# Layer 1 of a two-layer graph network: the fp16 halves of the attention probabilities formed per head from the exponentials, without a normalised fp32 copy

## The reference, cut to what matters

```python
def _L1_gnn_ref(x, adjacency_mask, Wq, Wk, Wv, Wo, bo):     # HEADS = 4, DIM_HEAD = 64
    q, k, v = split_heads(x @ Wq), split_heads(x @ Wk), split_heads(x @ Wv)
    sim = einsum('bhid,bhjd->bhij', q, k) * scale
    sim = where(adjacency_mask[:, None], sim, neg)
    attn = softmax(sim, axis=-1)
    out = einsum('bhij,bhjd->bhid', attn, v) ...
    return out @ Wo + bo
# x: (128 graphs, 128 nodes, 512).  Layer 0 (another attention, 8 heads) comes first:
x = x + _L0_gnn_ref(relu(layernorm(x)), adj, ...)
x = x + _L1_gnn_ref(relu(layernorm(x)), adj, ...)
```

## Time and profile before

| | |
|---|---|
| time, median of 3 runs | 2702.32 us (2700.8 to 2704.07) |
| the profiled execution | 2702.11 us, its span 2700.3 us |
| layer 1 in the trace | from about 1811 us to the end |
| busy over the span | PE 2599.2 us (96%), DVE 1982.8 (73%), ACT 1751.2 (65%), POOL 1403.3 (52%) |
| mean granted TensorE clock | 0.982 |

### The profile page before, as it was taken

One profiled execution on the slowest core, in us unless ns is written; L12 is line 12 of the kernel. 1 busy time (PEld: TensorE's weight loads), 2 busy tenths in 40 slices (PEclk: granted clock), 3 DMA queues, 4 the chain that ended last, 5 costly groups with the idle time before them and its releaser, 6 DMA issues. The chain is left out here.

```text
span 2700.3 us, 62494 instructions
## 1 busy us (share of the span) xinstructions
PE 2599.2 (96%) x20882; PEld 1398.8 (52%) x20886; DVE 1982.8 (73%) x6359; ACT 1751.2 (65%) x5020; POOL 1403.3 (52%) x2798
## 2 busy tenths in 40 slices
PE   7999999999999999999999999947999999999998
PEld 3455555555555555555555555533555555555554
DVE  5477777777777877777777778655777777777765
ACT  3566666666666666666666666645777777777774
POOL 4254555455545555555555455514655656555552
PEclk9999999999999999999999999968999999999998
DMA  4367666766766676667666766675777877777773
GB/s 139 66 142 150 134 135 142 147 131 135 150 146 136 131 150 147 129 138 154 139 132 140 155 128 131 120 174 113 159 165 160 171 163 165 167 159 170 155 149 91
DMA packets 944336, 385.33 MB, mean 143 GB/s; under 512 B 857488, under 2 KB 859024, under 8 KB 944016
## 3 DMA queue, kind: packets, MB, share of 16 engines
q1 hardware_dynamic: 944016, 381.34, 66.7%
HBM read 112.76 MB, written 67.11 MB: 67 GB/s over the span
## 5 line engine op out<-in xcount | busy, mean ns | idle before, releaser
L535 ACT ACTIVATE probs<-probs,negmax 128x128 f32<-128x128 f32 x1024 | 398.2, 390 | 468.4 <-DVE negmax L121 468.4
L446 POOL TENSOR_TENSOR o_sb<-o_sb,xres 128x512 f32<-128x512 f32 x128 | 162.7, 1271 | 503.5 <-DVE o_sb L694 498.3
L163 PE MATMUL ps_pj<-wm_hi,hT 128*128 128x512 f16 x1024 | 326.6, 381 | 14.2 <-DVE m_sb L637 7.3
L163 PE MATMUL ps_pj<-wv_hi,hT 128*128 128x512 f16 x1024 | 326.4, 380 | 0.0
L163 PE MATMUL ps_pj<-hT,wk_hi 128*128 128x512 f16 x1024 | 305.8, 380 | 0.0
L163 PE MATMUL ps_pj<-hT,wq_hi 128*128 128x512 f16 x1024 | 304.5, 379 | 0.0
L1231 ACT ACTIVATE l_probs<-l_probs,l_negmax 128x128 f32<-128x128 f32 x512 | 199.1, 390 | 153.8 <-DVE l_negmax L121 153.8
L1167 POOL TENSOR_TENSOR l_h<-l_h 128x512 f16<-128x512 f32 x124 | 143.6, 1158 | 271.7 <-ACT l_h L1210 190.8
L121 DVE CUSTOM_DVE_ANT_0 probs<-ps_sc,mask 128x128 f32<-128x128 f32 x1024 | 235.5, 284 | 52.2 <-PE ps_sc L900 52.2
L676 DVE SCALAR_TENSOR_TENSOR c<-cprobs,c 128x512 f16<-128x512 f32 x256 | 183.0, 715 | 81.2 <-ACT c L542 81.1
L542 ACT ACTIVATE c<-cprobs 128x512 f16<-128x512 f32 x256 | 160.3, 626 | 122.0 <-DVE cprobs L670 118.3
(11 more groups left out here) (197 smaller groups left out, 6665.8 us busy)
## 6 DMA issues: line engine op xcount, KB each, us to landing
xg<-in_x SPq DMA_DIRECT2D x128, 256.0 KB, 3.3
xres<-in_x SPq DMA_DIRECT2D x128, 256.0 KB, 3.0
x_scratch<-o_sb SPq DMA_DIRECT2D x128, 256.0 KB, 2.4
out<-l_o_sb SPq DMA_DIRECT2D x128, 256.0 KB, 3.3
room<-x_scratch SPq DMA_DIRECT2D x124, 256.0 KB, 3.1
cpT<-c SPq DMA_TRANSPOSE x256, 3.2
hT<-h SPq DMA_TRANSPOSE x128, 3.3
mask_u<-in_adj SPq DMA_DIRECT2D x32, 64.0 KB, 2.4
```

The costliest lines, as they stand in the source:

```text
L163: last = pe.matmul(out, a(kt), b(kt), start=(n == 0), stop=(n == 3 * kts - 1))
L446: nc.gpsimd.tensor_tensor(o_sb[:, j % 2], o_sb[:, j % 2], xres[:, j % 2], ALU.add).then_inc(res_done, 1)
L535: last = nc.scalar.activation(probs[:, i], probs[:, i], ACT.Exp, bias=negmax[:, u % 2, i:i + 1], scale=-1.0, accum_out=zsum[:, u % 4, hh:h ...
```

## The change

The multiplication by the reciprocal moves out of `normalise` into the two steps that write fp16. `normalise` becomes `reciprocals`: one small operation scales the four row sums by 2^-14, a second takes the reciprocal, with a semaphore wait between them. `p_high` becomes four instructions, one per head, that read `probs` with the head's reciprocal as a per-partition scale. `p_low` becomes four instructions of the same kind. The tile `nprobs` and its semaphore `np_done` go; `probs` and `rec` get two buffers, and `row_max(n)` now waits for `p_low(n-2)`.

```diff
-        rec = sb("rec", [P, HB])
-        probs = sb("probs", [P, HB, P])
-        nprobs = sb("nprobs", [P, HB, P])
+        rec = sb("rec", [P, 2, HB])
+        probs = sb("probs", [P, 2, HB, P])
...
             def exps(n):
                 act.wait_ge(negmax_done, count(n + 1))
-                act.wait_ge(np_done, count(n))
                 for hh in range(HB):
-                    last = nc.scalar.activation(probs[:, hh], probs[:, hh], ACT.Exp, bias=negmax[:, n % 2, hh:hh + 1], scale=-1.0,
+                    last = nc.scalar.activation(probs[:, n % 2, hh], probs[:, n % 2, hh], ACT.Exp, bias=negmax[:, n % 2, hh:hh + 1], scale=-1.0,
                                                 accum_out=zsum[:, n % 2, hh:hh + 1])
                 last.then_inc(exp_done, 1)
 
             def p_high(n):
-                act.wait_ge(np_done, count(n + 1))
+                act.wait_ge(rec_done, count(2 * n + 2))
                 act.wait_ge(pT_loaded[n % 2], 16 * (n // 2))
-                nc.scalar.activation(p16[:, n % 2, 0], nprobs[:], ACT.Copy, scale=F16_SCALE).then_inc(phi_done, 1)
+                for hh in range(HB):
+                    last = nc.scalar.activation(p16[:, n % 2, 0, hh], probs[:, n % 2, hh], ACT.Copy, scale=rec[:, n % 2, hh:hh + 1])
+                last.then_inc(phi_done, 1)
...
             def row_max(n):
                 if n % QUAD == 0:
                     dve.wait_ge(mask_ready, count(n // QUAD + 1))
-                dve.wait_ge(np_done, count(n))
-                mask_scores(nc, dve, s_ready, count(n + 1), probs, ps_s, mask[:, n // QUAD % 2, n % QUAD],
+                dve.wait_ge(plo_done, count(n - 1))
+                mask_scores(nc, dve, s_ready, count(n + 1), probs[:, n % 2], ps_s, mask[:, n // QUAD % 2, n % QUAD],
                             negmax[:, n % 2]).then_inc(negmax_done, 1)
 
-            def normalise(n):
+            def reciprocals(n):
                 dve.wait_ge(exp_done, count(n + 1))
-                nc.vector.reciprocal(rec[:], zsum[:, n % 2]).then_inc(rec_done, 1)
-                dve.wait_ge(rec_done, count(n + 1))
-                nc.vector.tensor_tensor(nprobs[:], probs[:], rec[:].unsqueeze(2).to_broadcast([P, HB, P]),
-                                        ALU.mult).then_inc(np_done, 1)
+                nc.vector.tensor_scalar(rec[:, n % 2], zsum[:, n % 2], 1.0 / F16_SCALE, None, ALU.mult).then_inc(rec_done, 1)
+                dve.wait_ge(rec_done, count(2 * n + 1))
+                nc.vector.reciprocal(rec[:, n % 2], rec[:, n % 2]).then_inc(rec_done, 1)
 
             def p_low(n):
                 dve.wait_ge(phi_done, count(n + 1))
-                nc.vector.scalar_tensor_tensor(p16[:, n % 2, 1], nprobs[:], F16_SCALE, p16[:, n % 2, 0], ALU.mult,
-                                               ALU.subtract).then_inc(plo_done, 1)
+                for hh in range(HB):
+                    last = nc.vector.scalar_tensor_tensor(p16[:, n % 2, 1, hh], probs[:, n % 2, hh], rec[:, n % 2, hh:hh + 1],
+                                                          p16[:, n % 2, 0, hh], ALU.mult, ALU.subtract)
+                last.then_inc(plo_done, 1)
```

More of the change, by code:

```diff
@@ L1075, in layer1 @@
             sem(n) for n in ("relu_done", "hhi_done", "q_done", "k_done", "vhi_done", "exp_done", "phi_done", "ahi_done")]
-        hlo_done, vlo_done, negmax_done, rec_done, np_done, plo_done, alo_done, out_done = dve_sems = [
-            sem(n) for n in ("hlo_done", "vlo_done", "negmax_done", "rec_done", "np_done", "plo_done", "alo_done", "out_done")]
+        hlo_done, vlo_done, negmax_done, rec_done, plo_done, alo_done, out_done = dve_sems = [
+            sem(n) for n in ("hlo_done", "vlo_done", "negmax_done", "rec_done", "plo_done", "alo_done", "out_done")]
         mask_ready, res_ready = pool_sems = [sem("mask_ready"), sem("res_ready")]
@@ L1356, in _ @@
             row_max(0)
-            normalise(0)
+            reciprocals(0)
             p_low(0)
@@ L1368, in _ @@
                 if n + 1 < B:
-                    normalise(n + 1)
+                    reciprocals(n + 1)
                 if n + QUAD < B:
```

## The result

| | before | after |
|---|---|---|
| time, median of 5 runs | 2701.71 us (2698.89 to 2704.07) | 2713.73 us (2710.13 to 2715.53) |
| ratio | | 1.0041, 95% interval 1.0029 to 1.0052 |
| span of the profiled execution | 2700.3 us | 2713.7 us |

A forecast was written before the change was run, and what follows sets the result against it. PE was taken to set the pace at 6.51 us per graph, waiting only at quad starts. Stalls +13.4, tail +2.3 and start +1 gave +16.7 on 2702.1: 2718.8 us, say 2718 (2714 to 2728; 8 in 10: 2706 to 2731).

The forecast's parts named there:

- lag: Time from the start of a graph's scores (PE) to the start of its row maximum (DVE); the least is 0.89 us.
- Prices: After the exponentials, four-piece p_high takes 1.26 against 0.63 us, and four-piece p_low 1.16 against 0.69, ending 0.57 later than before.
- E: The moment a graph's exponentials end, with the read of the last sum; p_high and p_low are timed from it.
- The threshold: At the copy of K before a quad's first scores: PE is not made to wait up to a fourth-graph lag of 1.52.
- The lag falls by 1.0 per graph: Kernel before: DVE and ACT together need about 5.5 us per graph against PE's period of 6.51, so DVE catches up.
- ladder: DVE and ACT steps from row maximum through p_low and add_residual to the next row maximum: 5.5 us before, 6.08 after.
- The held operation: In each quad's third graph POOL keeps the new small scaling waiting: 0 to 1.2 us, taken as 0.75; lag grows 0.32.
- Start and tail: Layer 1's first ladders cost +1 us (-0.5 to +1.5); four unhidden tail cycles cost 4 x 0.57 = +2.3.
- The sum: Quad-start stalls of 14.9 us less today's 1.5 give +13.4; with tail +2.3 and start +1, +16.7 in all.
- (a): Rival: the scaling slips between POOL's operations, no hold; +6.8 us, 2709, range 2707 to 2714; chance 0.24.
- (b): Rival: POOL's release shortens the long store waits, no quad stalls, not slower, 2703 or below; chance 0.16.
- (c): Rival: POOL's small operations cut into p_low's pieces in second graphs, up to four times 0.2 us; 2731; chance 0.10.

The follow-up runs named there:

- four tiles: Four output tiles l_o_sb instead of two, so add_residual does not wait for a store: on the kernel before 0.9992, on the changed kernel 1.0002.
- the store first: The changed kernel with SP issuing the store of a quad's fourth iteration ahead of transpose_h: 1.0007 of the kernel before.
- head by head without scaling: The changed kernel with p_low starting per head, and without the 2^-14 multiplication of the row sums (wrong result): 1.0000 of the kernel before.
- head by head: The changed kernel with p_low starting on a head as soon as p_high finished it: 1.0016 of before; with four output tiles too, 0.9986.

## Why the prediction was right, point by point

- **What bounds the kernel.** Right: PE sets the period of 6.51 us, the loss is PE's waits at the starts of quads, and they come from a lag that begins with a store. The runs with four tiles and with the store first show it: take the lag away and the stalls go.
- **Prices.** p_high was to end at E+1.70 and ended at E+1.73; p_low at E+2.89 and ended at E+2.90. Four pieces of p_low took 1.14 against the 1.16 of the sum. The figure from the Trainium skill, "Vector Engine (DVE) Microarchitecture Reference", section "Measured stream behaviour on trn2" (about 75 ns per instruction after overlap, from which 0.9 was estimated), did not hold for this form with its per-partition scale; with a constant scale the four took 0.90.
- **The threshold.** A lag of 1.52 in the fourth graph: in the trace after, a lag of 1.49 (graph 19) made no stall and 1.66 (graph 27) made one of 0.15.
- **The third graph before.** "The lag falls by 1.0 per graph" does not hold for third graphs. There POOL held the multiplication into nprobs and p_low already in the kernel before, so p_low ended at E+2.91 on average, and the lag fell by 0.82 from second to third graph but by only 0.07 from third to fourth (in many fourth graphs it was at its least). In graph 62, with POOL's operations of the earlier trace rows under way, the two took 1.06 and 0.98 instead of 0.69:

```profile
2263.50 1.06 DVE L1314 TENSOR_TENSOR l_nprobs<-l_probs,l_rec 128x512 f32<-128x512 f32 x1
...
2265.26 0.98 DVE L1319 SCALAR_TENSOR_TENSOR l_p<-l_nprobs,l_p 128x512 f16<-128x512 f32 x1
```

  After the change p_low ends at E+3.10 there. So the ladder grew by only 0.19 in third graphs, and by 0.56 to 0.63 in the others.
- **The held operation.** The step was right in kind and wrong in size, and it is the term that made the sum too high. I put 0.75 into each third graph; it was 0.20. I had said that POOL would be somewhat earlier and DVE later, and took a value near the old h_low; in truth DVE came 0.9 into xres and met only its end. The lag fell by 0.54 from the second to the fourth graph instead of 0.11. By the prediction's own sum 0.20 gives stalls from a lag of 2.18 on: 7.1 - 1.5 + 2.3 + 1 = +8.9, which is 2711.
- **A term that was missing.** I carried the second graphs' lags over unchanged (2.19). They rose to 2.38, and graph 111 met a second store wait of 0.75, which is part of the 2.1 us stall at graph 112. With the lags of the trace after in the same sum, 8.9 stands in place of 7.1: +10.7, or 2713. The rise does not come from a later store: SP's transpose_h waits for PE, so the store is issued 2.2 us ahead of the second graph's scores before and after. On average it took 3.74 from issue to landing instead of 3.57. It took 3.74 as well in the kernel before with four tiles, and the lag was 2.34 head by head without scaling, with the shortest ladder of all. So the rise does not follow the length of the ladder; what makes the landing time vary stays open.
- **Start and tail.** +1 was put in; from the scores of graph 0 to those of graph 9 it takes 0.9 more, as it does between the two kernels with four tiles. +2.3 was put in for the tail, 2.8 were measured, of which 4 x 0.58 is the ladder (12.16 against 11.01 for two cycles).
- **The sum.** 13.4 us of stalls were foreseen; the stalls to graph 112 grew by 9.4 (7.3 + 2.1). Scores(109) - scores(9) was to be near 666 and was 659.8. The total is +12.0 in the medians, +13.4 in the spans, between the forecast's +16.7 and the +6.8 of rival (a). 2713.7 lies in the range given for 8 in 10 runs, but just under the 2714 from which the forecast's own range begins. Two terms were off in opposite directions, the hold by 7.8 us too much and the second graphs' lags by 1.8 too little, and the store wait in graph 111 made up part of the rest; that the total is within 5 us of the forecast is in part luck.
- **The rivals.** (a), no hold, had 2707 to 2714: the time falls into it, but the hold was there, so it was right for a mixed reason. (b), that POOL's relief shortens the waits for the store, fell: POOL was relieved (410 to 360 us busy) and SP waited less for it, yet the lags did not fall, because the order in SP's queue and PE's project_v, for which transpose_h waits there, set when the store is issued. (c), p_low cut into by POOL's small operations, cost 0.05 (p_low ended at E+2.95 in second graphs), not 0.6.

## What to carry to other kernels

An engine that is 70% busy can still cost time if its steps stand in a chain with another's: count the ladder from the first to the last step, with the steps' waits, against the period, not the busy time. When one instruction is cut in four, let the next engine start after the first piece, or the cut lengthens the chain by the sum of both. And before paying for a faster chain, look at what makes it late: here one store moved ahead of a transpose in the same queue won back 8.6 of the 8.8 us that PE waited for.

## What the runs showed of the hardware

A VectorE tensor_scalar of four fp32 columns took 171 ns alone and up to 1152 ns when a GpSimd operation was under way. In the five kernels of layer 1 that have it, it took over 200 ns 171 times, and each time it ended within 0.04 us of the end of a GpSimd operation: 162 times xres, which has two inputs in SBUF, eight times the conversion of a mask, which has one, and once h_low. A reciprocal of the same four columns took at most 181 ns in all eleven traces. So how long the small operation lasts depends on when it comes: in third graphs mostly 0.37 in the change, up to 1.15 head by head, and mostly 0.53 in both of these with four output tiles and in the change with the store first. The multiplication of 128x512 into nprobs, with two inputs in SBUF, took 0.69 us alone and up to 1.79 when GpSimd was busy (kernel before with p_low in four).
